# Row maxima of causal attention in 17 units a group instead of 18, with a new interleaving, on one Trainium2 core

## The reference

```
xn = layernorm(x)
Q, K, V = xn @ wq.T, xn @ wk.T, xn @ wv.T      # 16 heads of 16 features
Q, K = rope(Q), rope(K)
scores = Q @ K.T / 4, masked so that a query sees no later key
s = softmax(scores) @ V @ wo.T
g = silu(ffn(xn))                              # gate/up/down, hidden 768, integer weights / 127
out = x + s * g
```

## Time and profile before

| | |
|---|---|
| runs | 1220.21, 1222.15, 1223.28 us; median 1222.15 us |
| profiled execution | 1219.1 us (its span from first to last instruction; the profile holds no other time of it) |
| instructions | 29979 |
| TensorE busy | 1176.2 us, 96% |
| VectorE busy | 971.1 us, 80% |
| ScalarE busy | 880.6 us, 72% |
| GpSimd busy | 638.2 us, 52% |

### The profile page before, as it was taken

How to read it: one execution, slowest core, us unless ns; L and a number is a source line. 1 busy time by engine, 2 the same in 40 slices (tenths; PEclk the granted TensorE clock), 3 DMA queues, 4 the chain that set the end, 5 groups by cost and what they waited for, 6 DMA issues and landing times.

```text
span 1219.1 us, 29979 instructions
## 1 busy us (share of the span) xinstructions
PE 1176.2 (96%) x10707; PEld 554.8 (46%) x10707; DVE 971.1 (80%) x1160; ACT 880.6 (72%) x1123; POOL 638.2 (52%) x996
## 2 busy tenths in 40 slices
PE   5999999999999889999999999999999999999997
PEld 3565556656555333334444443444444444444333
DVE  6666666667777689988898899889888988898843
ACT  4554554454444588788888888888888888888884
POOL 5765665765564322444455445554565455445554
PEclk9999999999999899999999999999999999999998
DMA  9755454566642511332323313333144133332122
GB/s 254 191 173 155 141 187 135 157 191 172 167 136 87 147 45 46 98 79 72 97 76 110 97 46 106 73 103 97 49 122 113 45 98 88 97 97 58 59 71 88
DMA packets 157888, 134.81 MB, mean 111 GB/s; under 512 B 49472, under 2 KB 142144, under 8 KB 157760
## 3 DMA queue, kind: packets, MB, share of 16 engines
q1 hardware_dynamic: 157760, 133.08, 38.7%
HBM read 72.61 MB, written 50.33 MB: 101 GB/s over the span
## 4 chain that ended last, share of the span: by engine, by line
PE 61%; ACT 2%; DVE 1%; issue 1%; POOL 1%; ACTq 0%; DVEq 0%; POOLq 0%
PE ps L1380 23%; PE ps L1363 14%; PE ps L794 12%; PE ps L1410 4%; PE ps L802 3%; PE ps L1394 3%; PE ps L1402 2%; ACT pr L1281 1%; DVE mxp L818 1%; PE ps L833 1%; ACT on L1293 0%; POOL ah L1101 0%; POOL zt L1119 0%; DVE yt L1219 0%; ACT ot L1288 0%
## 5 line engine op out<-in xcount | busy, mean ns | idle before, releaser
L818 DVE TENSOR_REDUCE mxp<-ps 128x2 f32<-128x1024 f32 (+2 forms) x576 | 685.3, 1221 | 91.0 <-PE ps L802 50.6
L1281 ACT ACTIVATE pr<-ps 128x1024 f32<-128x1024 f32 x576 | 575.8, 1023 | 100.5 <-PE ps L1363 86.1
L1380 PE MATMUL ps<-pr,vt 128*32 128x512 f32 (+3 forms) x3072 | 315.3, 497 | 0.6 <-POOL pr L1091 0.5
L1363 PE MATMUL ps<-qs,ks 50*128 50x512 f16 (+3 forms) x1536 | 225.6, 329 | 8.6 <-DVE mxp L818 4.2
L794 PE MATMUL ps<-ks,qs 48*128 48x512 f16 (+2 forms) x1792 | 225.2, 304 | 8.2 <-ACT pr L1281 4.8
L1091 POOL TENSOR_SCALAR_AFFINE_SELECT pr<-pr 128x256 f32<-128x256 f32 (+1 forms) x448 | 191.6, 454 | 51.3 <-ACT pr L1281 51.0
L1363 PEld LDWEIGHTS ps<-qs,ks 50*128 50x128 f16 x1536 | 65.4, 93 | 212.7 <-issue 201.6
L674 PE MATMUL ps<-xTh,wguT 128*128 128x512 f16 x384 | 145.8, 380 | 1.2 <-ACT vs L558 1.1
L674 PE MATMUL ps<-xTl,wguT 128*128 128x512 f16 x384 | 145.5, 379 | 0.0
L794 PEld LDWEIGHTS ps<-ks,qs 48*128 48x128 f16 x1792 | 83.0, 94 | 98.6 <-issue 85.0
L849 POOL TENSOR_SCALAR mp<-mneg 32x128 f16<-32x128 f32 x32 | 9.3, 289 | 206.3 <-issue 200.9
(11 more groups left out here) (104 smaller groups left out, 1355.9 us busy)
## 6 DMA issues: line engine op xcount, KB each, us to landing
v_d<-vs SPq DMA_DIRECT2D x16, 1024.0 KB, 5.3
vt<-v_d SPq DMA_DIRECT2D x32, 512.0 KB, 4.0
xs<-in_L_attn_x SPq DMA_DIRECT2D x16, 512.0 KB, 4.5
q_parts_d<-parts SPq DMA_DIRECT2D x16, 512.0 KB, 3.0
k_parts_d<-parts SPq DMA_DIRECT2D x16, 512.0 KB, 3.1
gate_d<-gs SPq DMA_DIRECT2D x16, 512.0 KB, 3.2
qs<-q_parts_d SPq DMA_DIRECT2D x64, 128.0 KB, 3.1
ks<-k_parts_d SPq DMA_DIRECT2D x64, 128.0 KB, 3.1
```

What stands on the lines that cost most here:

```text
L818: dve.tensor_reduce(dst, ps[:, slot:slot + 2, :].rearrange("p t (n s) -> p (t n) s", s=w), axis=AX.X, op=ALU.max).then_inc(keep["max_dve"] ...
L1281: act.activation(probs(step, s).rearrange("p (t j) s -> p t j s", t=2)[:, :, hs[0]:hs[-1] + 1, 0:w], ps[:, slot:slot + 2, 0:w * len(hs)].r ...
L1363: ins = pe.matmul(ps[:, slot + t, o:o + w], ks[g][r, j, kb * P:(kb + 1) * P], qs[g][r, j, lo:lo + w], start=o == 0, stop=True, skip_group_ ...
L1380: ins = pe.matmul(ps[VW * j:VW * (j + 1), O0, lo - c * CH:CH], vt[g % 2][:, kb, j, :], probs(step, s)[:, j, at:at + w], start=first, stop= ...
```

## The change

Maxima come in 17 units instead of 18. Let a query block have 128 rows. Its keys up to the middle of its diagonal block are now one piece; the last 64 keys, which only the block's lower 64 query rows can see, are taken out of it.

- **Long units** (8, for j = 0, 1 and the pairs of blocks (7, 4), (6, 5), (3, 0), (2, 1)): the tail of a long row and of a short one together make 512 columns (448 + 64 or 320 + 192). The mask covers the last 64 columns of each piece, in one matmul for each t of 2 x 64 columns.
- **Whole units** (8): the first 512 keys of blocks 7, 6, 5, 4, no mask.
- **Corners** (1, unit 7): the lower right 64 x 64 corner of all 8 diagonal blocks of all four heads. It takes 32 matmuls of 64 stationary and 64 moving columns; j selects the output's upper or lower 64 partitions, t the bank. One mask matmul for each t of 512 columns follows.
- **Maxima** of long and corner units are taken per 64 columns (16 results a row), into a wider `mxp`; the join is two reductions, of 8 slots and of 4. The corners of j = 0 lie on the wrong partitions; SyncE moves them by a new DMA (`move_corners`), and a new VectorE maximum of 64 x 32 elements (`top_max`) merges the corners. `transpose_max` waits for that.
- **Order**: 35 turns. `slot_of` now counts turns over groups, since 35 is not a multiple of 3. The corners come at turn 0, directly after the P @ V of turn 34 of the group before. The tile transpose TR[1] moves to turn 25, beside `MAXT`; the P @ V of step 9 moves to turn 7, beside TR[0]. Other work of ScalarE, VectorE and GpSimd is moved by up to five units.
- **First phase**: 24 peeked units instead of 25; the one at `down2` is gone.

```diff
@@ -35,9 +35,10 @@
 TILE = 64
 PAIR = 2
 SLOTS = 3
-SLOTS_Q = 3
 MASKED = -3.0e38
 LOADS = 16 * 8
+MATES = (2, 1), (3, 0), (6, 5), (7, 4)
+LONG, SHORT = 8, 4
 EXP_BITS = 0x7F800000
 TARGET = 4
 LEAST = 32
...
@@ -715,10 +714,11 @@
 
 WRITTEN_OUT = 3
 SHIFT = 7
+CORNERS = 7
 FFN_PLACES = "ffn1", "ffn2", "ffn3", "ffn4"
-PLACES = (((3, 1), FFN_PLACES), ((2, 0), FFN_PLACES), ((2, 1), FFN_PLACES), ((1, 0), FFN_PLACES + ("down0", "down2")),
+PLACES = (((3, 1), FFN_PLACES), ((2, 0), FFN_PLACES), ((2, 1), FFN_PLACES), ((1, 0), FFN_PLACES + ("down0",)),
           ((1, 1), ("q1", "k0") + FFN_PLACES + ("down0",)))
-PEEKED = [((0, 0), u) for u in range(18)] + [((0, 1), u) for u in range(SHIFT)]
+PEEKED = [((0, 0), u) for u in range(17)] + [((0, 1), u) for u in range(SHIFT)]
 PEEKS = {}
 for chunk, places in PLACES:
     PEEKS[chunk] = {place: PEEKED[sum(len(p) for p in PEEKS.values()) + n] for n, place in enumerate(places)}
...
@@ -752,17 +752,13 @@
 
 def query_units():
 
-
-    units = []
-    for qb in (7, 3, 6, 5, 4):
-        for j in range(PAIR):
-            for lo in range(0, (qb + 1) * P - CH + 1, CH):
-                units.append((lo // CH, [(j, qb, lo, CH)]))
-    for qb, lo, slot in ((1, 0, 0), (5, CH, 1), (6, CH, 1), (2, 0, 0)):
-        units.append((slot, [(j, qb, lo, 2 * P) for j in range(PAIR)]))
-    for (q0, lo0), (q1, lo1), slot in (((0, 0), (4, CH), 1), ((2, 2 * P), (6, 6 * P), 2)):
-        units.append((slot, [(j, q, lo, P) for j in range(PAIR) for q, lo in ((q0, lo0), (q1, lo1))]))
-    return units
+    parts = lambda qb: qb * P % CH + TILE
+    units = [("corners", 0, [])]
+    for j in range(PAIR):
+        units += [("long", j, [(a, a * P // CH * CH, parts(a)), (b, b * P // CH * CH, parts(b))]) for a, b in MATES[::-1]]
+    for qb in (7, 6, 5, 4):
+        units += [("whole", j, [(qb, 0, CH)]) for j in range(PAIR)]
+    return units[1:1 + CORNERS] + units[:1] + units[1 + CORNERS:]
 
 
 def load_stacks(sp, keep, parts_d, step):
...
@@ -785,51 +781,89 @@
     if u == 0:
         pe.wait_ge(keep["qk_ld"][g], (b + 1) * LOADS)
     hold(pe, held)
-    at, pieces = query_units()[u]
-    w = pieces[0][3]
-    masked = [lo + w == (qb + 1) * P for j, qb, lo, w in pieces]
-    for n, (j, qb, lo, w) in enumerate(pieces):
+    kind, j, pieces = query_units()[u]
+    if kind == "corners":
+        for qb in range(QB):
+            for half in range(PAIR):
+                for t in range(2):
+                    r, lo = slice(t * TILE, t * TILE + STACK), qb * P + TILE
+                    pe.matmul(ps[half * TILE:(half + 1) * TILE, slot + t, qb * TILE:(qb + 1) * TILE], qs[r, half, lo:lo + TILE],
+                              ks[r, half, lo:lo + TILE], start=qb == 0, stop=False, skip_group_check=True)
+    at = 0
+    for qb, lo, w in pieces:
         for t in range(2):
             r = slice(t * TILE, t * TILE + STACK)
-            ins = pe.matmul(ps[:, slot + t, n * w:(n + 1) * w], qs[r, j, qb * P:(qb + 1) * P],
-                            ks[r, j, lo:lo + w], start=n == 0, stop=not any(masked), skip_group_check=True)
-    if any(masked):
-
-        for half in range(2):
-            for t in range(2):
-                r = slice(t * TILE, (t + 1) * TILE)
-                o = ps[:, slot + t, :].rearrange("p (n s) -> p n s", s=w)[:, :, w - P + half * TILE:w]
-                ins = pe.matmul(o, pick[r, half ^ t, :], future[r, half ^ t, 0:len(pieces), half * TILE:P],
-                                start=False, stop=half == 1, skip_group_check=True)
+            ins = pe.matmul(ps[:, slot + t, at:at + w], qs[r, j, qb * P:(qb + 1) * P],
+                            ks[r, j, lo:lo + w], start=at == 0, stop=kind == "whole", skip_group_check=True)
+        at += w
+    if kind != "whole":
+
+        for t in range(2):
+            r = slice(t * TILE, (t + 1) * TILE)
+            blocks = ps[:, slot + t, :].rearrange("p (n s) -> p n s", s=TILE)
+            first = pieces[0][2] // TILE - 1 if pieces else 0
+            last = blocks[:, first::QB - 1 - first] if pieces else blocks
+            n = len(pieces) or QB
+            ins = pe.matmul(last, pick[r, t if pieces else 2, :], future[r, 0:n, t * TILE:(t + 1) * TILE],
+                            start=False, stop=True, skip_group_check=True)
     ins.then_inc(keep["max_pe"].sem, 1)
 
 
 def maximum(dve, ps, keep, step, u, slot):
 
-    at, pieces = query_units()[u]
-    j, qb, lo, w = pieces[0]
-    n = 2 * len(pieces)
-    per = GH * QB // n
+    kind, j, pieces = query_units()[u]
+    par = step[1] % 2
     if u == 0:
         dve.wait_ge(keep["mx_join"].sem, keep["mx_join"].after(earlier(step, 2)))
     dve.wait_ge(keep["max_pe"].sem, keep["max_pe"].after(step, u + 1))
-    first = ((j * QB) + qb) * SLOTS_Q + at
-    dst = keep["mxp"][step[1] % 2].rearrange("p h q s -> p (h q s)")[:, first:first + (n - 1) * per * SLOTS_Q + 1:per * SLOTS_Q]
-    dve.tensor_reduce(dst, ps[:, slot:slot + 2, :].rearrange("p t (n s) -> p (t n) s", s=w),
-                      axis=AX.X, op=ALU.max).then_inc(keep["max_dve"].sem, 1)
+    if kind == "corners":
+        dve.wait_ge(keep["mx_top"].sem, keep["mx_top"].after(earlier(step, 2)))
+        dve.tensor_reduce(keep["corner"][par][:, 1].rearrange("p t q -> p (t q)"), ps[:, slot:slot + 2, :].rearrange("p t (n s) -> p (t n) s", s=TILE),
+                          axis=AX.X, op=ALU.max).then_inc(keep["max_dve"].sem, 1)
+        return
+    qb = pieces[0][0]
+    mate = [m for m, qbs in enumerate(MATES) if qb in qbs][0]
+    dst = keep["mxp"][par].rearrange("p (t j) m s -> p t j (m s)", j=PAIR)[:, :, j]
+    if kind == "whole":
+        first = mate * (LONG + SHORT) + (0 if qb == MATES[mate][0] else LONG + SHORT - 1)
+        dve.tensor_reduce(dst[:, :, first], ps[:, slot:slot + 2, :], axis=AX.X, op=ALU.max).then_inc(keep["max_dve"].sem, 1)
+    else:
+        first = mate * (LONG + SHORT) + LONG - pieces[0][2] // TILE
+        dve.tensor_reduce(dst[:, :, first:first + CH // TILE], ps[:, slot:slot + 2, :].rearrange("p t (n s) -> p t n s", s=TILE),
+                          axis=AX.X, op=ALU.max).then_inc(keep["max_dve"].sem, 1)
 
 
 def join_max(dve, keep, step):
 
     par = step[1] % 2
+    src, dst = keep["mxp"][par], keep["mxa"][par].rearrange("p (h q) -> p h q", h=GH)
     dve.wait_ge(keep["mx_t"].sem, keep["mx_t"].after(earlier(step, 2)))
     dve.wait_ge(keep["max_dve"].sem, keep["max_dve"].after(step))
-    dve.tensor_reduce(keep["mxa"][par][:, :], keep["mxp"][par].rearrange("p h q s -> p (h q) s"), axis=AX.X,
-                      op=ALU.max).then_inc(keep["mx_join"].sem, 1)
+    dst = dst.rearrange("p h (x q) -> p h x q", x=2)
+    for qbs, at, n in ((slice(2, 4), 0, LONG), (slice(1, None, -1), LONG, SHORT)):
+        dve.tensor_reduce(dst[:, :, :, qbs], src[:, :, :, at:at + n].rearrange("p h (x m) s -> p h x m s", x=2), axis=AX.X,
+                          op=ALU.max).then_inc(keep["mx_join"].sem, 1)
+
+
+def top_max(dve, keep, step):
+
+    par = step[1] % 2
+    mxa = keep["mxa"][par].rearrange("p (t j q) -> p t j q", t=GH // PAIR, j=PAIR)[TILE:P]
+    corner = keep["corner"][par].rearrange("p j t q -> p t j q")[TILE:P]
+    dve.wait_ge(keep["mx_move"].sem, keep["mx_move"].after(step))
+    dve.wait_ge(keep["mx_join"].sem, keep["mx_join"].after(step))
+    dve.tensor_tensor(mxa, mxa, corner, ALU.max).then_inc(keep["mx_top"].sem, 1)
+
+
+def move_corners(sp, keep, step):
+
+    par = step[1] % 2
+    sp.wait_ge(keep["max_dve"].sem, keep["max_dve"].after(step, CORNERS + 1))
+    sp.dma_start(keep["corner"][par][TILE:P, 0], keep["corner"][par][0:TILE, 1]).then_inc(keep["mx_move"].sem, 16)
 
 
 def transpose_max(pe, ps, keep, step, bank, at=0):
-    pe.wait_ge(keep["mx_join"].sem, keep["mx_join"].after(step))
+    pe.wait_ge(keep["mx_top"].sem, keep["mx_top"].after(step))
     pe.matmul(ps[0:GH * QB, bank, at:at + P], keep["mxa"][step[1] % 2][:, :], keep["ident"][:, :],
               start=True, stop=True).then_inc(keep["mx_t"].sem, 1)
 
...
@@ -938,15 +972,15 @@
                 out += [(nth(step, 2), u) for u in range(SHIFT)]
             return out
 
-        def slot_of(turn):
-
-            return 2 * (turn % SLOTS)
-
-
-        ORDER = "EMEMEMEMEMEMEEMEMEMMEMEMEMEMEMEMEMEM"
+        def slot_of(step, turn):
+
+            return 2 * ((step[0] * NG + step[1]) * TURNS + turn) % (2 * SLOTS)
+
+
+        ORDER = "MEEMEMEMEMEMEEMEMMEMEMEMEMEMEMEEMME"
         E_TURN, M_TURN = ([t for t, kind in enumerate(ORDER) if kind == k] for k in "EM")
         TURNS = len(ORDER)
-        assert TURNS % SLOTS == 0 and len(E_TURN) == NU and len(M_TURN) == NM
+        assert len(E_TURN) == NU and len(M_TURN) == NM
 
         def wait_slot(pe, step, turn):
 
...
@@ -1003,14 +1038,15 @@
                 return pr[(step[1] * NSTEP + s) % PROBS]
 
 
-            V_AT = (9, 12, 16, 23, 27, 30, 35, TURNS + 1, TURNS + 4, TURNS + 6)
+            V_AT = (9, 12, 16, 23, 27, 30, TURNS - 1, TURNS + 1, TURNS + 4, TURNS + 7)
```

(34 more changed lines are left out.)

26 lines of the change are left out of this document (12 added, 14 removed).

## The result

The changed kernel is slower: 1232.77 us (1230.71 to 1234.92, 4 runs) against 1221.53 us (1220.21 to 1223.28, 4 runs), a ratio of 1.0091, 95% interval 1.0078 to 1.0104. I had forecast 1196. The profiled execution spans 1229.0 us, 9.9 more than before.

A forecast was written before the change was run, and what follows sets the result against it. TensorE was taken as the bound; columns and corners, -0.72 us a set over 32 sets (-23.0), plus tiling changes (-3.1) gave -26.1 us, from 1222.15 to 1196 us, range 1188 to 1211.

The forecast's parts named there:

- Score and mask columns, -0.43 and -0.64: TensorE, per set of maxima: two score units fewer save 0.43 us, 1536 fewer mask columns for each t save 0.64.
- Corners, 0.35: TensorE: the 32 new 64 x 64 corner matmuls add 0.35 us a set, taken between 0.21 and 0.46.
- Rivals A: Corner matmuls on TensorE: only two run at once, 0.80 us a set, 1210 us in all; chance 0.12.
- B (1.82): Corner matmuls on TensorE: unhidden weight loads, 57 ns each, 1.82 us a set, 1243 us in all; chance 0.06.
- the estimate of 0.43 us from the Trainium skill's price of a plain weight load: Corner matmuls: eight rounds each waiting 53 ns for plain loads, 0.43 us, total 2.6 us less favourable.
- Tiling changes, -0.10: TensorE's array tiling: net one change fewer a group, -0.10 us in 31 groups, -3.1 us.
- VectorE's work and the corners' transfer: VectorE does 0.7 us less a group beside TensorE, priced at nothing; the corners' DMA has 6 us margin, cost nothing.
- Rival D: SyncE's corner transfer lands late and holds up `top_max`; needs over 6 us more than seen, slower; chance 0.03.
- Moved work. I take 0 here, with -0.2 to +0.4 us a group: VectorE and ScalarE take two units in a row at new neighbours, other work moves by turns: no cost expected.
- Rival C: Score slots not yet read when neighbouring units want them: +0.4 us a group, 12 us, 1208 us; chance 0.15.
- TensorE is the bound: Attention phase: TensorE, busy 99.8%, sets the 24.45 us group; VectorE and ScalarE about 2.5 us a group behind.

The follow-up runs named there:

- e2: Kernel before with P @ V of step 9 and the second tile transpose each moved one turn, beside other foreign blocks: 1225.74 us, ratio 1.0035.
- e9: Changed kernel with those two neighbour places parted again (P @ V of step 9 at turn 6, second tile transpose at 26): 1233.33 us, ratio to before 1.0102.
- e6: Kernel before without its mask matmuls, order, units and readers unchanged: 1214.11 us, ratio 0.994.
- e10: Changed kernel's units in another order of 35 turns with other places moved along: 1217.23 us, ratio to before 0.9967.

## Why the prediction was wrong, point by point

- **Score and mask columns, -0.43 and -0.64: right.** Columns a group fell by 0.85 us net, with the corners' own columns at 0.21.
- **Corners, 0.35: too dear.** They run four tiles at a time: 0.28 us for the 32. Rivals A (0.80) and B (1.82) are out. So is the estimate of 0.43 us from the Trainium skill's price of a plain weight load ("TensorE: Matmul & The Clock Gate", LDWEIGHTS): the rounds start 32 ns apart, where that price would keep them 53 ns apart.
- **Tiling changes, -0.10: right as a count, worthless as time.** 33 instead of 34. In e2 two fewer took 0.35 us out of the column of changes and in e9 two more put 0.50 in, waits included; the time did not follow in either. The rule of the Trainium skill that a change of the tiling mode drains the array ("TensorEngine Tiling (Array Packing)", Key Properties) agrees with the 0.10 to 0.16 us that each takes here when no engine is waited for.
- **VectorE's work and the corners' transfer: right.** Its share is 85%, the join costs 287 + 209 + 190 ns, and the transfer lands long before it is wanted. Rival D is out.
- **"Moved work. I take 0 here, with -0.2 to +0.4 us a group": this step failed.** The waits between score units grew by 1.39 us a group. Over 31 groups that is +43 us, against -31 us on columns and at tiling changes (0.85 + 0.16 a group): +12. The groups' own lengths say the same, 30 x 0.39 = 11.7 us, and about 2 us are gained back before and after them: 9.9. Rival C was the right mechanism at a third of its size: it had +0.4 and said that at +0.85 nothing would be left. One reading behind the 0 was wrong as well: I gave TensorE a P @ V of 1.00 us between M16 and M17, but the one that stands there has 256 columns and takes 0.57 (925.58 to 926.15), against 1.22 us of VectorE for a unit. And I looked at two of the places where two units of a kind follow each other; the new order has five.
- **Behind it, "TensorE is the bound".** I took the busy share of 99.8% for proof and the idle time of the readers, 2.5 us a group (2.9 for ScalarE), for room. Neither is. The modelled ends of the matmuls hide waits of 0.1 to 0.2 us, of which the kernel before had 0.7 us a group, and the readers' idle time did not let TensorE run ahead: e6 removed 1.28 us of TensorE's work and gained 0.19.

**What the order does.** From the rows after: a maximum's slot is held for 0.44 us (written and picked up, 925.26 to 925.70), 1.22 us (read) and about 0.15 us until TensorE writes again, 1.8 us; a second M in a row, at turn 17, holds its own for about 2.05 (926.15 to 928.20). Three score units are 0.66 us of TensorE. So between a unit and the third after it there has to be more than a microsecond of P @ V, projection or transposes, for each slot again. The old order alternates E and M but for two places (E at 12, 13; M at 18, 19). The new one has five (E at 1, 2; 12, 13; 30, 31; M at 16, 17; 32, 33), each of which asks one reader for two units running while the other has none. Two pairs of its 17 blocks of other matmuls stand next to each other, so that fewer stretches of score units are broken by one. In the stretch shown, the wait follows directly from such a pair: it is the 0.70 us of turn 20, where the kernel before waits 0.19. The other four pairs show little. Their slots come free before TensorE wants them, but for turn 15 (slot of E12, 0.24) and turn 34 (slot of E31, 0.04). The rest stands at single units in stretches with little other work, at turns 7, 12, 23, 27 and 30.

So two things are in the 1.39 us, the lighter work and the order. Their shares are an estimate. In e6, with the old order untouched, about 85% of the work taken from TensorE turned into waits. The same share of the 1.01 us saved here is 0.86. That leaves about 0.5 us for the new order, which is also what turn 20 waits more than before, and what e10 (24.37 us a group) is faster by. No run changes the pair M16, M17 alone, so this split is not shown.

## What to carry to other kernels

When producer and readers share a few buffers in a fixed order, take the time of one buffer's round (write, pick up, read, release) against what the producer does in as many turns, before pricing anything by the producer's busy share. A cheap test tells whether its work is worth time: take some away without touching the order (here the masks, -1.28 us for -0.19), and halve both readers, not one. Stretches of the same trace in which the producer has less to do are such a test for nothing: here the first batch. Fewer units mean a new order, and the order has to be priced too, not the units alone.

## What I had not expected of the hardware

- Thirty-two float16 matmuls of 64 x 64 with 48 rows, each with its own weight load, took 0.28 us on four tiles, about 9 ns each: the four of a round start 3 to 4 ns apart, the rounds 32 ns.
- A VectorE maximum of 128 x 1024 float32 out of PSUM costs 1220 ns with 2 results a row and with 16.
- After a reader has ended, TensorE's next matmul into its slot starts 0.14 to 0.15 us later, for VectorE and for ScalarE alike.
- Joining blocks to spare a tiling change saved the change and lost as much in waits (e2: -0.35, +0.47 us a group).
